# One 160-column product for the neighbours' values and tanh layer, and five turns instead of four ahead of the first aggregation

## What is computed

```python
mask = (adj > 0)
agg  = mask @ x / max(deg, 1)                        # 4096x4096 @ 4096x256
l0   = relu(concat(x @ W_self + b_self, agg @ W_nb + b_nb) @ W_comb + b_comb)
x    = layernorm(x + l0)
neib_att = tanh(neigh @ Wn1 + bn1) @ Wn2 + bn2       # 4096x256 @ 256x32 @ 32x32
value    = neigh @ Wv + bv                           # 4096x256 @ 256x128
x_att    = tanh(x @ Wx1 + bx1) @ Wx2 + bx2
ws   = softmax(where(mask, leaky_relu(x_att @ neib_att.T), -9e15), axis=1)
x    = layernorm(x + concat(x @ Wfx + bfx, ws @ value))
```

## Time and profile before

| | us |
|---|---|
| median of 3 runs | 730.77 (729.89 to 730.90) |
| the profiled execution, time | 730.62 |
| its span | 728.8 |
| PE busy | 689.6 (95% of the span) |
| DVE busy | 621.7 (85%) |
| ACT busy | 573.5 (79%) |
| PE on the chain that ended last | 86% |

### The profile page before, as it was taken

How to read it: one execution, slowest core, us unless ns; L and a number is a source line. 1 busy time by engine, 2 the same in 40 slices (tenths; PEclk the granted TensorE clock), 3 DMA queues, 4 the chain that set the end, 5 groups by cost and what they waited for, 6 DMA issues and landing times.

```text
span 728.8 us, 19763 instructions
## 1 busy us (share of the span) xinstructions
PE 689.6 (95%) x7344; PEld 592.1 (81%) x7344; DVE 621.7 (85%) x1535; ACT 573.5 (79%) x920; POOL 129.9 (18%) x242
## 2 busy tenths in 40 slices
PE   5989998999999999999999999999999999998775
PEld 4646676888888888888888888888888888886554
DVE  4887668999999999999999999999999999987874
...
DMA packets 260145, 141.39 MB, mean 194 GB/s; under 512 B 225361, under 2 KB 243665, under 8 KB 260049
## 3 DMA queue, kind: packets, MB, share of 16 engines
...
q10 hardware_dynamic: 444, 0.02, 0.0%
...
## 4 chain that ended last, share of the span: by engine, by line
PE 86%; ACT 5%; DVE 4%; issue 3%; POOL 1%; DMA 1%; SPq 0%; POOLq 0%; ACTq 0%
PE ps_v L1137 22%; PE ps_agg L1092 15%; PE ps_agg L1095 14%; PE ps_t L1116 10%; PE ps_s L1107 7%; PE ps_agg L1156 3%; PE ps_agg L1159 3%; PE ps_s L1006 2%; PE ps_v L1014 2%; PE ps_x L1176 1%; PE ps_x L1179 1%; ACT score L913 1%; PE ps_t L997 1%; PE ps_x L1023 1%; DMA neigh_sb<-in_L_gnn_neigh_dram 1%
## 5 line engine op out<-in xcount | busy, mean ns | idle before, releaser
L1092 PE MATMUL ps_agg<-x,mask_t 128*128 128x257 f16 x1024 | 243.4, 274 | 0.2 <-DMA mask_t<-mask 0.2
L1095 PE MATMUL ps_agg<-x,mask_t 128*128 128x256 f16 x1024 | 237.4, 273 | 0.3 <-DVE x L533 0.3
L907 ACT ACTIVATE score<-ps_s,sc 128x512 f32<-128x512 f32 x256 | 178.7, 698 | 63.1 <-PE ps_s L1107 57.6
L692 DVE CUSTOM_DVE_ANT_0 score<-score,mask 128x512 f32<-128x512 f32 x256 | 175.9, 687 | 16.7 <-ACT score L907 14.3
L1137 PEld LDWEIGHTS ps_v<-v,late 128*128 128x128 f16 x2304 | 143.9, 97 | 41.7 <-DVE late L756 16.9
L1137 PE MATMUL ps_v<-v,late 128*128 128x129 f16 (+1 forms) x2304 | 162.6, 219 | 11.6 <-DVE late L773 6.0
L913 ACT ACTIVATE score<-score,exp_bias,sc 128x1024 f32<-128x1024 f32 x128 | 159.4, 1246 | 3.2 <-DVE exp_bias L701 3.2
L756 DVE TENSOR_TENSOR late<-ps_t,late 128x512 f16<-128x512 f32 x192 | 130.7, 681 | 33.2 <-ACT late L920 31.4
L920 ACT CAST late<-ps_t 128x512 f16<-128x512 f32 x192 | 114.8, 598 | 20.4 <-PE ps_t L1116 20.4
L1116 PE MATMUL ps_t<-ident,score 128*128 128x128 f32 x768 | 116.8, 275 | 5.3 <-ACT score L913 5.1
L1095 PEld LDWEIGHTS ps_agg<-x,mask_t 128*128 128x128 fp8e4 x1024 | 100.3, 98 | 15.5 <-issue 5.2
...
## 6 DMA issues: line engine op xcount, KB each, us to landing
adj_sb<-in_adj_dram SPq DMA_DIRECT2D x128, 512.0 KB, 5.3
...
mask_t<-mask SPq DMA_TRANSPOSE x128, 4.8
neigh_sb<-neigh_sb SPq DMA_TRANSPOSE x64, 3.7
...
```

The source lines that it names most:

```text
L692: dve.tensor_tensor_reduce(score[:, b % 2, part], score[:, b % 2, part], mask[:, b % MASK_BUFS, part], 1.0, -3.0e38, ALU.subtract, ALU.max ...
L907: act.activation(score[:, b % 2, k * GW:(k + 1) * GW], ps_s[k % 2][:, :], ACT.Prelu, alpha=SLOPE, scale=score_scale).then_inc(leaky_made, 1)
L1092: mm = pe.matmul(agg[:, 0:D + 1], mask_t8[:, c, 0, :], x16[:, c, X_HI:X_ONE + 1], start=(c == 0), stop=(c == NC - 1), skip_group_check=True)
L1095: mm = pe.matmul(agg[:, 0:D], mask_t8[:, c, 0, :], x16[:, c, X_LO:X_LO + D], start=False, stop=False, skip_group_check=True)
```

## The change

- `neigh_values` and the two products of `neigh_hidden` become one: `neigh_products` takes a turn's transposed rows as weights and moves 160 columns (`wvh_sb`: 128 of Wv, 32 of Wn1), 8 matmuls a turn. The result takes two banks, viewed by `joint(turn)`: `agg_both` for turn 1, `s_both` for all the others.
- The 32 hidden columns arrive with rows in the partitions. ACT copies them out (`copy_h`, 128x128), PE transposes them in one instruction (`neigh_hidden`), and the tanh then runs on 128x128 instead of 32x512.
- The attention product takes 4 matmuls of 128 columns, each with a weight tile that is zero outside its 32 rows. POOL clears these tiles, DVE fills them with four copies instead of two.
- `PRE` is 5: turns 5, 6 and 7 stay in the loop. The order of the opening is written out anew on PE and ACT, and DVE has two more steps ahead of the masks of block 0.

```diff
...
@@ -88,7 +89,7 @@
-PRE = 4
+PRE = 5
 TURN_SLOTS = 3
 Z_BIAS_SLOT = 2
...
@@ -198,11 +199,17 @@
         wide_t = wide[:, :, 2:4, :].rearrange("p q a (c n) -> p q a c n", n=P)
+        def joint(turn):
+            both = agg_both if turn == 1 else s_both
+            return both[:, :, :].rearrange("p k (u n) -> p (k u) n", u=2)[:, :, 0:VH]
         def turned(turn, dc):
             return neigh_sb[:, TR * turn:TR * (turn + 1), dc * P:(dc + 1) * P]
-        wn2_sb = sb("wn2_sb", [H, H3], F32)
-        bn1_sb = sb("bn1_sb", [H, 1], F32)
+        wn2_sb = sb("wn2_sb", [P, H], F32)
+        bn1_sb = sb("bn1_sb", [P, 1], F32)
         bn2_sb = sb("bn2_sb", [P, 1], F32)
         z_bias = sb("z_bias", [P, D], F32)
         b_cols = sb("b_cols", [P, 2 * DC], F32)
...
@@ -559,9 +572,11 @@
                 power_below(p_xn, p_xn)
                 scale_link(dve.reciprocal(s_xn, p_xn))
                 scale_link(dve.tensor_scalar(s_xn, s_xn, TOP, None, ALU.mult))
-                scale_link(dve.tensor_scalar(wn2_sb[:, 0:H], wn2_sb[:, 0:H], s_xn[0:H, 1:2], None, ALU.mult))
-                for k in range(1, 3):
-                    dve.tensor_copy(wn2_sb[:, k * H:(k + 1) * H], wn2_sb[:, 0:H]).then_inc(att_copied, 1)
+                scale_link(dve.tensor_scalar(wn2_sb[:, :], wn2_sb[:, :], s_xn[:, 1:2], None, ALU.mult))
+                for u in range(TR):
+                    part = slice(u * H, (u + 1) * H)
+                    dve.tensor_copy(wn2_u[part, u, :].rearrange("p (k h) -> p k h", k=3),
+                                    wn2_sb[part, :].unsqueeze(1).broadcast_to((H, 3, H))).then_inc(att_copied, 1)
                 dve.tensor_scalar(bn2_sb[:, :], bn2_sb[:, :], s_xn[:, 1:2], None, ALU.mult).then_inc(bounds_scaled, 1)
             def scale_x_attention():
...
@@ -653,10 +668,12 @@
             dve.wait_ge(x_scanned, NT)
             dve.tensor_reduce(x_top, tops[:, 1, :], AX.X, ALU.max).then_inc(x_top_made, 1)
             n_low(2)
+            v_low(3)
             dve.wait_ge(x_top_reduced, 1)
             x_scale_chain()
-            v_low(3)
             x_low(0)
+            v_low(4)
+            n_low(3)
             for q in range(NQ):
                 make_mask(0, q)
...
@@ -822,16 +839,19 @@
                     act.wait_ge(rows_transposed, DC * turn + dc + 1)
                     act.copy(turned(turn, dc), ps_t[dc][:, :].rearrange("p (u n) -> p u n", u=TR)).then_inc(rows_t_copied, 1)
+            def copy_h(turn):
+                act.wait_ge(v_done, turn + 1)
+                at_least(act, h_done, turn)
+                act.copy(h_rows.rearrange("p (u h) -> p u h", u=TR), joint(turn)[:, :, DV:VH]).then_inc(h_copied, 1)
             def v_high(turn):
                 act.wait_ge(v_done, turn + 1)
-                act.activation(v16[:, TR * turn:TR * (turn + 1), 0:DV],
-                               ps_s[turn % 2][:, :].rearrange("p (u n) -> p u n", u=TR), ACT.Copy,
-                               scale=v_scale).then_inc(v_hi_made, 1)
+                act.activation(v16[:, TR * turn:TR * (turn + 1), 0:DV], joint(turn)[:, :, 0:DV], ACT.Copy, scale=v_scale).then_inc(v_hi_made, 1)
             def hidden(turn):
                 act.wait_ge(h_done, turn + 1)
                 at_least(act, natt_done, turn)
-                act.activation(h_t, ps_h[0:H, :], ACT.Tanh, bias=bn1_sb[:, 0:1]).then_inc(h_tanh, 1)
+                act.activation(h_t, ps_h[:, 0:P], ACT.Tanh, bias=bn1_sb[:, 0:1]).then_inc(h_tanh, 1)
             def n_high(turn):
                 act.wait_ge(natt_done, turn + 1)
@@ -847,39 +867,49 @@
             act.wait_ge(neigh_w_in, 16 * len(NEIGH_WEIGHTS))
             copy_rows_t(0)
             copy_rows_t(1)
+            copy_h(0)
             hidden(0)
             copy_rows_t(2)
-            hidden(1)
-            n_high(0)
+            copy_h(1)
             for k, w_t in enumerate((ws_t, wn_t)):
                 act.wait_ge(w_transposed, k + 1)
                 act.copy(w_t, ps_t[k][:, :]).then_inc(w_t_copied, 1)
+            hidden(1)
+            n_high(0)
             copy_rows_t(3)
             act.wait_ge(v_scaled, 1)
             v_high(0)
             v_high(1)
+            copy_h(2)
+            v_high(2)
+            n_high(1)
             for c in range(DC):
                 act.wait_ge(m_done, c + 1)
                 act.copy(m_both[:, c, :], ps_m[c][:, :]).then_inc(m_copied, 1)
-            v_high(2)
             hidden(2)
-            n_high(1)
-            copy_rows_t(PRE)
+            copy_rows_t(4)
+            copy_h(3)
             v_high(3)
             hidden(3)
             n_high(2)
+            copy_rows_t(PRE)
+            copy_h(4)
             x_high(0)
+            v_high(4)
+            hidden(4)
+            n_high(3)
             x_high(1)
             def first_part(s):
                 if s == 0:
                     n_high(PRE - 1)
                 if (t := turn_due(s, 0)) is not None:
-                    if t + 1 < NT:
-                        copy_rows_t(t + 1)
+                    copy_h(t)
                     v_high(t)
                 if (t := turn_due(s, 1)) is not None:
                     hidden(t)
+                    if t + 1 < NT:
+                        copy_rows_t(t + 1)
                 if (t := turn_due(s, 2)) is not None:
                     n_high(t)
                 if s + 2 < NT:
@@ -998,31 +1028,34 @@
                                           neigh_sb[:, TR * turn + u, dc * P:(dc + 1) * P], ident[:, :])
                     mm.then_inc(rows_transposed, 1)
-            def neigh_values(turn):
+            def neigh_products(turn):
                 pe.wait_ge(rows_t_copied, DC * (turn + 1))
-                at_least(pe, v_lo_made, turn - 1)
+                if turn >= 2:
+                    free = 1 if turn == 2 else turn
+                    pe.wait_ge(v_lo_made, free)
+                    pe.wait_ge(h_copied, free)
                 for u in range(TR):
                     for dc in range(DC):
-                        mm = pe.matmul(ps_s[turn % 2][:, u * DV:(u + 1) * DV],
-                                       turned(turn, dc)[:, u, :],
-                                       wv_sb[:, dc, :], start=(dc == 0), stop=(dc == DC - 1))
+                        mm = pe.matmul(joint(turn)[:, u, :], turned(turn, dc)[:, u, :],
+                                       wvh_sb[:, dc, :], start=(dc == 0), stop=(dc == DC - 1))
                 mm.then_inc(v_done, 1)
             def neigh_hidden(turn):
+                pe.wait_ge(h_copied, turn + 1)
                 at_least(pe, h_tanh, turn)
-                for dc in range(DC):
-                    mm = pe.matmul(ps_h[0:H, :], wn1_sb[:, dc, :], turned(turn, dc), start=(dc == 0),
-                                   stop=(dc == DC - 1))
-                mm.then_inc(h_done, 1)
+                pe.transpose(ps_h[:, 0:P], h_rows, ident[:, :]).then_inc(h_done, 1)
             def neigh_attention(turn):
                 pe.wait_ge(h_tanh, turn + 1)
                 at_least(pe, natt_lo, turn)
                 if turn == 0:
-                    pe.wait_ge(att_copied, 2)
-                pe.matmul(ps_x[0:H3, :], wn2_sb[:, :], h_t, start=True, stop=True).then_inc(natt_done, 1)
-
-            def combine_weights():
+                    pe.wait_ge(att_copied, TR)
+                for u in range(TR):
+                    mm = pe.matmul(ps_x[0:H3, u * P:(u + 1) * P], wn2_u[:, u, :], h_t, start=True, stop=True)
+                mm.then_inc(natt_done, 1)
+            def turn_weights():
                 pe.wait_ge(comb_in, 16 * len(COMB_WEIGHTS))
                 for k, w in enumerate((ws_raw, wn_raw)):
                     pe.wait_ge(rows_t_copied, DC * 2 + k + 1)
@@ -1031,8 +1064,11 @@
                             at = (kc * DC + dc) * P
                             mm = pe.transpose(ps_t[k][:, at:at + P], w[:, dc, kc * P:(kc + 1) * P], ident[:, :])
                     mm.then_inc(w_transposed, 1)
-                rows_turn(3)
+            def combine_weights():
                 pe.wait_ge(w_t_copied, 2)
+                pe.wait_ge(v_lo_made, 2)
+                pe.wait_ge(h_copied, 2)
                 for dc in range(DC):
                     for w_t, c0, col in ((wn_t, DC, 0), (ws_t, 0, D)):
                         for kc in range(DC):
@@ -1050,25 +1086,37 @@
                 mm.then_inc(m_done, 1)
             rows_turn(0)
-            for turn in range(PRE):
-                if turn != 2:
-                    rows_turn(turn + 1)
-                neigh_values(turn)
-                neigh_hidden(turn)
-                if turn > 0:
-                    neigh_attention(turn - 1)
-                if turn == 1:
-                    combine_weights()
+            rows_turn(1)
+            neigh_products(0)
+            rows_turn(2)
+            neigh_products(1)
+            neigh_hidden(0)
+            turn_weights()
+            neigh_hidden(1)
+            neigh_attention(0)
+            rows_turn(3)
```

(18 more changed lines are left out.)

30 lines of the change are left out of this document (17 added, 13 removed).

## The result

| | median us | range | runs |
|---|---|---|---|
| before | 730.75 | 729.89 to 732.03 | 9 |
| changed | 732.80 | 731.79 to 736.44 | 9 |

The ratio is 1.0035, 95% interval [1.0025, 1.0046]: the changed kernel is slower by 0.35%; the medians are 2.05 us apart. Forecast was 729.8 us. The forecast was 0.8 us less than before's profiled execution; the time lies on the other side of before, by more than the interval leaves open.

The account below looks back on a forecast made before the run. PE work was taken to bound the kernel, with gains possible only before block 0's combination at 82.15 us. Later aggregation +5.5, less slot work -9.0, new waits +2.7 gave -0.8: 729.8 us against 730.62, range 726.5 to 733.8.

Parts of the forecast that it names:

- The sum up to the combination of block 0: Opening and slots up to that combination's start (C0): 5.5 - 9.0 + 2.7 = -0.8 us, C0 at 81.3.
- P2's start: Opening on PE: turn 2's joint product waits for v_low(0), starting at 27.2 us after 3.9 us idle.
- A4: Opening on PE: turn 4's attention product reuses n_low(3)'s bank, starting at 48.8 us after 3.2 us idle.
- waits +2.7 net: Slots up to block 0's combination: new PE waits of 3.3 us together, less the 0.56 of before.
- What that costs ... all of P2 would be 2.2. I take 1.2: Opening: half clock behind the idle ahead of turn 2's joint product costs 1.2 us.
- I take 0.95 and 0.9: Ahead of aggregation: half clock costs turn 4's attention 0.95 us and turn 5's joint product 0.9 us.
- there PE's work is the time, and the change touches nothing of it: From 120 to 640 us: PE busy 520.00 of 520.00 us at granted clock 1.00, unchanged.
- masks of block 1: Slots up to block 0's combination: PE waits another 0.3 us for these masks.
- Rival A: Opening: low clock sooner and longer, from turn 4's joint product on; +2.7 us, 733.3; chance 0.22.
- Rival B: Opening: clock holds in the wait ahead of turn 4's attention, aggregation starts at 52.6; 728.0 us; chance 0.25.
- C: Rival on the slots up to block 0's combination: the new waits don't come; -3.5 us, 727.1; chance 0.13.
- D: Rival: the joint product costs as 256 columns do, 3.46 us for 5 products; +6 us, 736; chance 0.02.

Follow-up runs that it names:

- changed again: The changed kernel once more, unedited, as a second series with a new profile: median 732.18 us, ratio to before 1.0019.
- the execution at 736.44: The profiled execution of the changed kernel's first series, the highest of its nine, with the second turn's rows landing late: 736.44 us.
- P5 first: The changed kernel with turn 5's joint product ahead of turn 4's attention, ACT and DVE reordered likewise: 730.15 us, ratio to before 1.0005.
- joint with four: The changed kernel with PRE = 4, so four turns ahead of aggregation instead of five: 730.74 us, ratio to before 1.0004.
- masks first: The changed kernel with ACT's x_high(0) ahead of copy_h(4) and DVE's block 0 masks ahead of v_low(4) and n_low(3): 733.93 us, ratio to before 1.0057.
- half the loads: The changed kernel with the 12 loads of blocks 1 to 3 moving half their bytes, so another output: 730.90 us, ratio to before 1.0006.
- the five-ahead kernel with the old products: The kernel before with PRE = 5 and its old products: 730.95 us, ratio to before 1.0001.
- the filled ones: Variants with unused matmuls in PE's opening gaps; on the changed kernel, both gaps filled 726.59 us (0.9952 to before), the first alone 728.06 us (0.9966).
- the fill with transposes: The changed kernel with only the gap ahead of turn 2's joint product filled, by 28 transposes instead of 14 matmuls: 727.93 us, ratio to before 0.9978.

## Why the prediction was wrong

By its own steps, in changed again:

- *The sum up to the combination of block 0* (-0.8, C0 at 81.3): 81.35, right. Its parts: P2's start 27.2, measured 26.65; first mask 49.3, DVE starts them at 48.55 and the first is there some 0.6 later; P4 42.3, measured 41.85; A4 48.8, measured 48.67; waits +2.7 net, measured 1.74 + 0.34 + 1.43 = 3.51 less the same 0.56, +2.95 (with a small slip on the way: 45.9 + 1.2 + 0.7 + 0.75 is 48.55, not 48.65). P was taken as 2.24, measured 2.18 from start to start (35.88 to 38.06); copy_h 0.28, measured 0.27; tanh 0.40, measured 0.37.
- *"What that costs ... all of P2 would be 2.2. I take 1.2"*, and *"I take 0.95 and 0.9"* for A4 and P5. This is the term mis-sized. Measured: P2 +1.5 and A1 +0.2 in one execution, +2.2 and +0.4 in the other; A4 +0.9 and P5 +2.1 in both. So 4.7 to 5.6 us where 3.05 stood. Aggregation started at 54.7 us, not 53.8; that C0 came out right all the same is because the steps from there to C0 took 26.6 us instead of 27.5. About 0.5 of that is that in the slots A took 0.87 from start to start where 0.95 stood, H 0.11 for 0.17 and P 2.18 for 2.24. Two errors of 0.9 us cancelled, which was luck. In the execution at 736.44 C0 came at 84.81, 3.5 us later than in changed again: 2.5 of it is there when P2 starts (29.17), from the late rows, and the rest is the longer half clock of P2 and A1.
- *"there PE's work is the time, and the change touches nothing of it"*, and all shifts equally behind C0. This is the step that failed. True from combination 1 on (574.94 against 574.89 us) but not in the step before it: +1.67 us, the DMA supply. The time from the start of aggregation to C0 shrank by 7.2 us (33.80 to 26.64), while the loads and transposes of blocks 1 and 2 moved as many bytes as before and started later against C0. The priced wait for "masks of block 1", 0.3, was this mechanism, put one block too early and at a sixth of the loss.
- *The tail* was not looked at. It is +1.13: PE waits 0.64, 0.94 and 0.96 us for the transposes of the last blocks' p, which are issued as in before and land in 3.4 to 3.5 us (medians of two) where before has 2.8 to 3.1. From 668 to 726 us the same 9024 packets took 28.8% of the DMA engines' time where they took 19.0% in before. Such waits stand in the profiled executions of the changed kernel (both), P5 first, joint with four, masks first and half the loads; not in those of before, of the five-ahead kernel with the old products and of the filled ones. Its cause is open.
- *Rival A* had the side right (733.3, the clock low longer), and its second half, A4 and P5 at half clock throughout, came as priced. Its trigger, P4 behind 1.77 us of waiting, did not: P4 took 2.41. The rule of the Trainium skill ("TensorE: Matmul & The Clock Gate", part "PE-mode transpose") that transposes don't count as busy for the clock, which was to carry A, has no support here: the fill with transposes held P2's clock as matmuls do. *Rival B*, the clock holding, is what P5 first showed in one execution and the fills force. *C* fell: the waits that it left out came. *D* fell, P is 2.18 (and P2 to P7 are six products ahead of C0, not five).
- *The chances.* Slower had 0.25. With two places behind C0 unpriced and the clock's price varying from one execution to the next, more belonged there.
